# Attention scores as two products of 64 rows and 128 key columns each, with a reordered set-up

## The reference

```python
q = _split_heads(hidden_states @ w_q, HEADS)
k = _split_heads(text @ w_k, HEADS)
v = _split_heads(text @ w_v, HEADS)
out_text = _merge_heads(_sdpa(q, k, v))
mask_ip = _ip_mask(bbox, B, S, hidden_states.dtype)
k_ip = _split_heads(ip_h @ w_k_ip, HEADS)
v_ip = _split_heads(ip_h @ w_v_ip, HEADS)
out_ip = _merge_heads(_sdpa(q, k_ip, v_ip, mask=mask_ip))
out = (out_text + IP_SCALE * out_ip) @ w_out + b_out + residual
```

## Time and profile before

| | |
|---|---|
| median of 3 runs | 893.89 us (893.0 to 894.28) |
| the profiled execution's own time | 893.49 us |
| its span in the trace | 891.7 us |
| busy in the span: PE, PEld | 876.4 us, 749.5 us |
| busy: DVE, ACT, POOL | 725.7 us, 603.9 us, 540.6 us |
| instructions | 13892 |

### The profile page before, as it was taken

One profiled execution on the slowest core, in us unless ns is written; L12 is line 12 of the kernel. 1 busy time (PEld: TensorE's weight loads), 2 busy tenths in 40 slices (PEclk: granted clock), 3 DMA queues, 4 the chain that ended last, 5 costly groups with the idle time before them and its releaser, 6 DMA issues.

```text
span 891.7 us, 13892 instructions
## 1 busy us (share of the span) xinstructions
PE 876.4 (98%) x4685; PEld 749.5 (84%) x4685; DVE 725.7 (81%) x1006; ACT 603.9 (68%) x986; POOL 540.6 (61%) x431
## 2 busy tenths in 40 slices
PE   7999999999999999999999999999999999999988
PEld 6889788888888888888888888888888888888866
DVE  7959579787887979887897979888897979888784
ACT  7556486775758586675858587675858587675753
POOL 5349769284664839285664929375574929475561
PEclk9999999999999999999999999999999999999999
DMA  9843312203030301203030200303030210300011
GB/s 303 292 166 112 103 44 78 79 1 133 1 126 1 125 8 31 94 0 132 0 125 0 100 32 9 116 0 132 0 125 0 77 55 0 118 25 36 1 59 60
DMA packets 34059, 64.63 MB, mean 72 GB/s; under 512 B 4464, under 2 KB 6512, under 8 KB 33904
## 3 DMA queue, kind: packets, MB, share of 16 engines
q1 hardware_dynamic: 33888, 62.97, 21.0%
q10 hardware_dynamic: 144, 1.31, 0.3%
HBM read 40.34 MB, written 23.59 MB: 72 GB/s over the span
## 4 chain that ended last, share of the span: by engine, by line
PE 82%; DVE 4%; ACT 1%; POOL 1%; issue 0%; DVEq 0%
PE bank L95 23%; PE bank L97 22%; PE bank L96 22%; PE bank L1002 7%; PE bank L1011 4%; PE bank L1012 4%; DVE o_raw L905 1%; DVE res L912 1%; DVE total L223 1%; DVE pT_lo L898 1%; ACT oT_hi L820 0%; POOL prob L176 0%; ACT pv_part L816 0%; DVE prob L182 0%; DVE prob L176 0%
## 5 line engine op out<-in xcount | busy, mean ns | idle before, releaser
L765 POOL TENSOR_TENSOR oT_lo<-o_raw,oT_hi 128x512 fp32r<-128x512 f32 x80 | 103.5, 1293 | 244.1 <-ACT oT_hi L820 244.1
L176 POOL TENSOR_TENSOR prob<-prob,top 128x1120 f32<-128x1120 f32 x126 | 178.7, 1448 | 0.0
L182 POOL TENSOR_TENSOR prob<-prob,inv 128x1120 f32<-128x1120 f32 x126 | 174.1, 1414 | 0.2 <-DVE inv L225 0.2
L95 PE MATMUL bank<-xT_hi,wq_hi 128*128 128x512 f32 x400 | 163.3, 408 | 0.0
L97 PE MATMUL bank<-xT_hi,wq_lo 128*128 128x512 f32 x400 | 156.8, 392 | 0.0
L95 PE MATMUL bank<-oT_hi,wo_hi 128*128 128x512 f32 x400 | 156.2, 391 | 0.1
L96 PE MATMUL bank<-oT_lo,wo_hi 128*128 128x512 f32 x400 | 155.8, 389 | 0.0
L97 PE MATMUL bank<-oT_hi,wo_lo 128*128 128x512 f32 x400 | 155.7, 389 | 0.0
L96 PE MATMUL bank<-xT_lo,wq_hi 128*128 128x512 f32 x400 | 155.6, 389 | 0.0
L905 DVE TENSOR_TENSOR o_raw<-bank,pv_part 64x512 f32<-64x512 f32 x160 | 110.2, 689 | 50.7 <-ACT pv_part L816 48.2
L212 ACT ACTIVATE prob<-prob 128x1280 f32<-128x1280 f32 x64 | 81.6, 1276 | 79.7 <-POOL prob L176 79.6
(11 more groups left out here) (110 smaller groups left out, 1780.9 us busy)
## 6 DMA issues: line engine op xcount, KB each, us to landing
xin<-in_xT SPq DMA_DIRECT2D x16, 1280.0 KB, 6.8
outT<-res SPq DMA_DIRECT2D x80, 256.0 KB, 6.6
w_raw<-in_L_xattn_w_k SPq DMA_DIRECT2D x8, 320.0 KB, 5.6
w_raw<-in_L_xattn_w_k_ip SPq DMA_DIRECT2D x8, 320.0 KB, 5.5
w_raw<-in_L_xattn_w_v_ip SPq DMA_DIRECT2D x8, 320.0 KB, 3.1
w_raw<-in_L_xattn_w_v SPq DMA_DIRECT2D x8, 320.0 KB, 3.5
v_raw<-v_scratch SPq DMA_DIRECT2D x14, 140.0 KB
prob<-in_textT SPq DMA_DIRECT2D x8, 224.0 KB, 5.0
```

Of the source, the lines that this page charges most:

```text
L95: nc.tensor.matmul(dst, a_hi, b_hi, start=first, stop=False)
L176: ins = eng.tensor_tensor(s, s, top[:, t, n, :].unsqueeze(2).broadcast_to([P, HEADS, k1 - k0]), ALU.subtract)
L182: ins = eng.tensor_tensor(s, s, inv[:, t, n, :].unsqueeze(2).broadcast_to([P, HEADS, k1 - k0]), ALU.mult)
L765: nc.gpsimd.tensor_tensor(oT_lo[:, m, :], o_raw[:, m % 2, :], oT_hi[:, m, :].bitcast(F32), ALU.subtract).then_inc(oT_lo_done, 1)
```

## The change

The scores are made in two halves. A step's 128 rows are cut into rows 0 to 63 (heads 0 and 1 of the four) and 64 to 127 (heads 2 and 3). Each half is multiplied with only its own 128 key columns and writes a bank of its own, the two in turn. `k_hi` and `k_lo` become one tile `k_parts` [128, 5, 2 parts, 128 columns], of half the size. Four steps (`RUN`) fill one pair of banks, so PE's unit of work is now a pair of banks, five in a group (`score_units`), and ACT still copies ten banks of 512 columns, each into four strips of 128 columns of `prob` (`score_dst`). Pair u of 2 or more waits for `score_copied` of both banks of pair u-2. `units_for_tile` gives 4, 6, 8, 10 where it gave 3, 5, 8, 10.

In the set-up, PE does 20 transposes of the identity into bank 7 before its first wait for the context. The mask is split in two (`find_inside`, `make_mask`) and moved behind the low parts of query blocks 1 and 2; ACT's first copy of scores waits for it. Two of three `x_lo_part` of group 1 move behind the first and the second of the late weight chunks. POOL clears one key tile instead of two.

```diff
+    PW = 2 * KEYS
+    RUN = 512 // PW
...
-        k_hi, k_lo = sb("k_hi", [P, KD, HPT, KEYS], F32R), sb("k_lo", [P, KD, HPT, KEYS], F32R)
+        k_parts = sb("k_parts", [P, KD, 2, PW], F32R)
...
-            return -(-(t + 1) * SW // 512)
+            return 2 * -(-(t + 1) * KD // RUN)
...
-        def score_unit(pe, g, n, b, new_batch):
-            if n < 2:
+        def score_dst(n):
+
+            steps = prob[:, n // 2 * RUN * CW:(n // 2 + 1) * RUN * CW].rearrange("p (i r c) -> p r i c", r=2, c=PW)
+            return steps[:, n % 2, :, :]
+
+        def score_units(pe, g, u, b, new_batch):
+            if u == 0:
                 wait(pe, score_copied, UNITS * g)
-            elif n < 4:
+            elif u == 1:
                 wait(pe, pT_lo_done, PAIRS * g)
             else:
-                pe.wait_ge(score_copied, UNITS * g + n - 3)
-            if n == 0 and new_batch:
+                pe.wait_ge(score_copied, UNITS * g + 2 * u - 2)
+            if u == 0 and new_batch:
                 pe.wait_ge(k_built, HPT * (b + 1))
-            for half in range(2):
-                t, m = divmod(2 * n + half, KD)
+            for i in range(RUN):
+                t, m = divmod(RUN * u + i, KD)
                 if t == 0:
                     pe.wait_ge(q_lo_done, KD * g + m + 1)
                 q_cols = slice(t * P, (t + 1) * P)
-                keys = [k[:, m, :, :].rearrange("p j k -> p (j k)") for k in (k_hi, k_lo)]
-                ins = three(s_bank[n % 4][:, half * CW:(half + 1) * CW], qT_hi[:, m, q_cols], qT_lo[:, m, q_cols], *keys, True, True)
-            ins.then_inc(score_ready, 1)
...
+                for n, (q, part) in enumerate(((qT_hi, 0), (qT_hi, 1), (qT_lo, 0))):
+                    for r in range(2):
+                        rows = slice(r * HP, (r + 1) * HP)
+                        ins = nc.tensor.matmul(s_bank[(2 * u + r) % 4][:, i * PW:(i + 1) * PW], q[rows, m, q_cols], k_parts[rows, m, part, :], start=n == 0, stop=n == 2)
+                        if i == RUN - 1 and n == 2:
+                            ins.then_inc(score_ready, 1)
...
+                    act.wait_ge(mask_step, 6)
                     for u in range(UNITS):
                         copy_scores(act, 0, u)
...
-                            if k == KC - 3:
-                                make_mask()
...
                         q_lo_part(dve, 0, m)
+                        if m == 1:
+                            find_inside()
+                        elif m == 2:
+                            make_mask()
...
-                    for k in range(2, KD):
-                        x_lo_part(dve, 1, 1, k)
-                    for c in behind[4:]:
+                    x_lo_part(dve, 1, 1, 2)
+                    for n, c in enumerate(behind[4:]):
                         lo_chunk(c)
+                        if n < 2:
+                            x_lo_part(dve, 1, 1, 3 + n)
...
+                    pe.wait_ge(ident_made, 1)
+                    for n in range(20):
+                        nc.tensor.transpose(bank[7][:, 0:P], ident[:], ident[:])
```

More of the change, by code:

```diff
@@ L127, in q_lo_part, with k_head @@
             nc.vector.tensor_tensor(qT_lo[:, m, :], l_bank[(m + 1) % 2][:], qT_hi[:, m, :].bitcast(F32), ALU.subtract).then_inc(q_lo_done, 1)
-        def k_head(t, j):
-            return t[j * DH:(j + 1) * DH, :, j, :]
+        def k_head(part, j):
+            return k_parts[j * DH:(j + 1) * DH, :, part, j % 2 * KEYS:(j % 2 + 1) * KEYS]
         def k_hi_part(act, b, raw=None):
@@ L136, in k_hi_part @@
             for j in range(HPT):
-                nc.scalar.activation(k_head(k_hi, j), raw[j * DH:(j + 1) * DH], ACT.Copy).then_inc(k_hi_built, 1)
+                nc.scalar.activation(k_head(0, j), raw[j * DH:(j + 1) * DH], ACT.Copy).then_inc(k_hi_built, 1)
         def k_lo_part(dve, b, raw=None):
@@ L198, in score_unit, with copy_scores @@
                 q_cols = slice(t * P, (t + 1) * P)
-                keys = [k[:, m, :, :].rearrange("p j k -> p (j k)") for k in (k_hi, k_lo)]
-                ins = three(s_bank[n % 4][:, half * CW:(half + 1) * CW], qT_hi[:, m, q_cols], qT_lo[:, m, q_cols], *keys, True, True)
-            ins.then_inc(score_ready, 1)
-        def copy_scores(act, g, u):
-            act.wait_ge(score_ready, UNITS * g + u + 1)
-            nc.scalar.activation(prob[:, u * 512:(u + 1) * 512], s_bank[u % 4][:], ACT.Copy).then_inc(score_copied, 1)
+                for n, (q, part) in enumerate(((qT_hi, 0), (qT_hi, 1), (qT_lo, 0))):
[4 more added lines that the diff above has]
+                            ins.then_inc(score_ready, 1)
+        def copy_scores(act, g, n):
+            act.wait_ge(score_ready, UNITS * g + n + 1)
+            nc.scalar.activation(score_dst(n), s_bank[n % 4][:].rearrange("p (i c) -> p i c", c=PW), ACT.Copy).then_inc(score_copied, 1)
         def exponentials(act, g, t, shared):
@@ L386, in _ @@
                                             pattern=[[-1, P]], channel_multiplier=1).then_inc(ident_made, 1)
-                    for buf in (k_hi, k_lo):
-                        nc.gpsimd.memset(buf[:].rearrange("p m j k -> p (m j k)").bitcast(F32), 0.0).then_inc(k_zeroed, 1)
+                    nc.gpsimd.memset(k_parts[:].rearrange("p m s c -> p (m s c)").bitcast(F32), 0.0).then_inc(k_zeroed, 1)
                     mine = [c for c in range(len(chunks)) if c % 2 == 1]
@@ L516, in lo_chunk, with step, find_inside @@
                         nc.vector.tensor_tensor(lo, w_raw[:, c % LOADS, :], hi.bitcast(F32), ALU.subtract).then_inc(w_lo_done[0], 1)
[L518 to L524, removed]
+                    def step(ins, n):
+                        ins.then_inc(mask_step, 1)
+                        dve.wait_ge(mask_step, n)
+                    def find_inside():
                         def edge(f, cols=None):
@@ L534, in make_mask @@
                         nc.vector.tensor_tensor(inside_y[:, 0, :, :], y_all, edge(1, TPB), ALU.is_ge)
[L535 to L537 removed]
+                        step(nc.vector.tensor_tensor(inside_y[:, 1, :, :], y_all, edge(3, TPB), ALU.is_le), 1)
+                        step(nc.vector.tensor_tensor(inside_x[:, 0, :], inside_x[:, 0, :], inside_x[:, 1, :], ALU.mult), 2)
+                        step(nc.vector.tensor_tensor(inside_y[:, 0, :, :], inside_y[:, 0, :, :], inside_y[:, 1, :, :], ALU.mult), 3)
                         ins_all = inside[:].rearrange("p b m t -> p (b m) t")
[L539 to L540 removed]
+                        nc.vector.tensor_tensor(ins_all, inside_y[:, 0, :, :], inside_x[:, 0, :].unsqueeze(2).broadcast_to([P, B * BOXES, TPB]), ALU.mult).then_inc(mask_step, 1)
+                    def make_mask():
+                        dve.wait_ge(mask_step, 4)
+                        step(nc.vector.tensor_reduce(any_in, inside[:].rearrange("p b m t -> p b t m"), AX.X, ALU.max), 5)
                         mask_b = mask[:].rearrange("p (b t) k -> p b t k", b=B)
@@ L544, in make_mask @@
                             last = nc.vector.tensor_scalar(mask_b[:, :, :, BOXES + n], inside[:, :, n, :], 1.0, -NEG, ALU.subtract, ALU.mult)
-                        step(last)
+                        last.then_inc(mask_step, 1)
                     mine = [c for c in range(len(chunks)) if c % 2 == 0]
@@ L679, in _ @@
                             ins.then_inc(k_ipT_ready, 1)
-                    for n in range(UNITS):
-                        score_unit(pe, 0, n, 0, True)
+                    for u in range(UNITS // 2):
+                        score_units(pe, 0, u, 0, True)
                     for k in range(KC):
@@ L1038, in scores @@
                 def scores(g, b, new_batch, more):
-                    for n in range(UNITS):
-                        score_unit(pe, g, n, b, new_batch)
+                    for u in range(UNITS // 2):
+                        score_units(pe, g, u, b, new_batch)
                     for m in range(KD):
```

4 lines of the change are left out of this document (2 added, 2 removed).

## The result

| | before | after |
|---|---|---|
| median | 893.58 us (893.0 to 897.21, 20 runs) | 894.89 us (894.39 to 895.76, 20 runs) |
| profiled execution, its span | 893.49 us, 891.7 us | 894.63 us, 892.8 us |

The ratio is 1.0013 with a 95% interval of 1.0007 to 1.0019: 1.3 us slower, where 890.0 and a gain were forecast. The time lies inside the range of 866 to 900, and inside the 0.2% that the prediction called no difference, but the interval shows a small loss.

What follows compares the result with a forecast made beforehand. PE, busy 98% of the span, was taken as the bound. From the profiled 893.5 us, 0.5 for the halves and 3.4 for the set-up gave 889.6; with the median 0.4 above, 890.0 us, range 866 to 900.

Steps and rivals of the forecast that it cites:

- The pace of a pair: PE's scores: time from one pair of half matmuls to the next, taken as 0.11 us, against 0.120 per matmul before.
- (d): Rival on PE's scores: full doubling, a pair every 0.06 us, ACT's copies bind, 866.5 us; chance 0.12.
- (c): Rival on PE's scores: pairs at the old pace of 0.12 us, 0.36 more a group, 896.3 us; chance 0.15.
- (b): Rival on PE's scores: loads of the halves run one after the other, 0.22 us a pair, 991 us; chance 0.22.
- Going in and out: PE entering and leaving 64-row matmuls around the scores: 0.29 us extra a group, lower bound 0.
- the waits for copies: PE's score pairs waiting for ACT to copy banks: 0.06 and 0.21 us, 0.27 a group.
- the halves bring 0.03 a group: Score stage on PE: 7.16 us a group against 7.19, a gain of 0.5 us in 16 groups.
- The chain ends 0.36 later, and 1.09 was there.: Softmax chain: POOL's mask of tile 2 starts 0.36 us later, inside POOL's 1.09 us lead over PE's transposes.
- The set-up: Before group 0: 2.0 us from an earlier quick pace and 1.4 from late weights, 3.4 gained, bounds 0 and 3.6.
- The late weights: Set-up: two subtractions of x moved behind DVE's low part of weights, which PE awaits 1.41 us; 1.4 us gained.
- Rival (a): Rival on the set-up: the transposes don't raise the clock, 2.0 us are missing, 892.0 us; chance 0.15.
- The prediction's rival on the other side: PE's scores: loads one after the other, 6.3 us more a group, 991 us; chance 0.22.

Runs made afterwards that it cites:

- half of the terms: Changed kernel without the two low-order products of rows 64 to 127, four matmuls a step instead of six; 957.79 us in one run.
- Keys late: Changed kernel with DVE's next-batch key subtractions moved behind the low parts of the first two query blocks and two pT_part; 891.14 us, ratio 0.9969 to the kernel before.
- halves in turn: Changed kernel with three matmuls of one half issued, then three of the other, in each step; 894.52 us in one run.
- the set-up alone: Kernel before with only the set-up edits (20 transposes, mask and two x subtractions moved), scores as before; 890.37 us, ratio 0.9962.
- the halves alone: Changed kernel with the set-up of before, so only the scores in halves; 898.03 us, ratio 1.0046 to the kernel before.

## Why the prediction went wrong

**The pace of a pair was right**, 0.112 us for 0.11. The bounds of 0.06, 0.12 and 0.22, rivals (d), (c) and (b), are all out. Loads of the two halves run side by side, a load of 64 rows is recorded as long as one of 128 (0.19 us), and the work of one half binds (half of the terms); that its loads are what binds is the prediction's reason, and nothing here speaks against it. The Trainium skill (TensorEngine Tiling (Array Packing), Key Properties) says that different tiles can execute weight loads and matmuls in parallel; the trace agrees, with two loads within 0.19 us. It gains nothing more here, since each half has to load as often as the whole did.

**Going in and out, and the waits for copies.** 0.29 + 0.27 a group were forecast. The waits are 0.05 and 0.16 in group 5, 0.2 in all. Going in costs 327.31 - 326.99 = 0.32 against a pace of 0.23, and the first pairs stand 0.05 further apart; leaving costs 0.09 and 0.10: 0.34 together. With 20 steps of 0.335, 6.70 where 6.60 were forecast, the sum is 7.2. From steady matmul to steady matmul it is 7.70 less two steps of 0.23, 7.24, where the earlier trace rows have 7.19 and the forecast 7.16. So "the halves bring 0.03 a group" should have read: they cost 0.05, 0.8 us in 16 instead of 0.5 gained. It is a term mis-sized by 1.3 us: the edges (0.34 for 0.29) and a pace of 0.112 for 0.110 sixty times over add 0.15 a group, the waits take back 0.06.

**The failed step** is "The chain ends 0.36 later, and 1.09 was there." The 0.36 was right (0.40). The cover of 1.09 is that of POOL's scaling before PE's transposes in group 5, and in groups 1 to 14 it held: PE has no wait for `prob` there. It failed in two ways. The same 0.36 moves DVE's sums, DVE's order puts four key subtractions and then `qT_lo` behind them, and in seven groups PE was already late by that, 0.13 us each; the 0.37 more in each are 2.6 us. And in the last group there was no cover: PE waited 0.32 for POOL and now waits 0.64, and the end comes 0.35 later. With the 0.05 of the halves themselves in 15 groups (0.8) these make 3.7 of the 3.9 us lost behind the set-up. The rest lies in the groups without new keys, which are 0.10 longer and not 0.05; the new waits for `res` of DVE stand there, but no run priced them. So from the first transposes on the kernel lost 3.9 where 0.5 less was forecast, 4.4 of the 5.0 us between the 889.6 forecast for the profiled execution and its 894.63; the set-up is the other 0.6. Keys late takes the wait for `qT_lo` away and gets 3.75 us back, of which 7 x 0.50 = 3.5 are priced by the groups.

**The set-up** was right in kind. 2.8 us came of 3.4. The quick pace came at 7.3 instead of 6.9, and the transposes brought 1.2 us where 2.0 were counted: 12 slow matmuls were to be saved, but between the two set-ups, with and without the transposes, it was 2.7 us of slow time (7.6 against 10.3), 7 matmuls at 0.16 each. The 5.3 us of work that stood ahead of the quick pace in the kernel before is no constant: in the other traces it was 3.1 (halves in turn) to 6.1 us (the set-up alone). The mask, which the sum put at nothing, brought some of the rest: PE stands 1.7 us ahead of the kernel before at the end of the first 15 matmuls and 2.5 ahead at about 64 us, before the late weights. The late weights brought some 0.4 instead of 1.4: PE begins them 1.4 us earlier, and then waits 0.74 for POOL's low part, which was hidden behind DVE's. Rival (a), that the transposes don't raise the clock, fell. The Trainium skill (TensorE: Matmul & The Clock Gate, PE-mode transpose) says that transposes don't count as busy in the same way; here the measurement decides otherwise, quick pace at 7.6 with 20 of them ahead and at 10.3 without, and in halves in turn at 4.6, among the transposes themselves.

**The chances.** The case that came was the forecast one in its mechanism, with an addition that none of the rivals named. The prediction's rival on the other side needed a mishap on PE; the one that happened was 0.36 us of delay on an engine that looked 81% busy. That 894.89 lies inside the range, and nearer to the 896.3 of rival (c) than to the forecast, is luck: (c) asked for pairs at 0.12, and they went at 0.112.

**Open.** In the profiled executions two kernels with halves have short stretches at a lower clock that the others don't show: 0.83 in 90 to 100 us and 0.84 in 860 to 870 us of the halves alone, 0.85 in 860 to 870 us of keys late. Over all executions with both halves at full work, 9 of 37 have a mean granted clock of 0.998 or less; of the 46 with the scores in one piece none has. So the stretches come with the halves, though why isn't shown. They don't explain the loss: the profiled execution of the changed kernel kept 1.00, and its four executions at 0.998 (894.5 to 895.35) are no slower than the others. In the halves alone the two such executions are the slowest of five (898.83 and 900.27), so there they may cost something.

## What to carry to other kernels

A cover belongs to one pair of engines and to one kind of group; the last group, with less work ahead of the same wait, may have none. When a chain ends later, follow every consumer of it, engine by engine and in each kind of group, to the work that stands behind it in a fixed order; the row to look for is the instruction that starts just as its input is ready, with no wait shown yet. Work that is needed a stage later (here the next batch's keys) should not stand ahead of work that another engine is about to need. Splitting a matmul's rows gained little here, 0.112 us for 0.120, since every half needs its own loads, and going in and out cost more than that.

## What the runs showed of the hardware

- Two fp32r matmuls of 64 rows and 128 columns in different row halves and banks, with their loads, take 0.112 us a pair. Their order in the queue, in turn or three and three, changes nothing, and taking away two of one half's three changes nothing either (0.335 us for three in all three kernels).
- Where one half of the rows did a third of its matmuls (one execution), the granted clock fell below 0.8 in some 10 us of nearly every group, to 0.50 at the end of the score stage shown, and 957.8 us were measured for less work. The profiled execution of the changed kernel, with both halves working, kept 1.00. An experiment that takes work off PE can be slower by the clock alone, so its clock is to be read before its time.
- DVE's subtraction of 32 x 320 elements took 1.04 us on average, 0.49 to 2.25, while POOL was scaling (28 in 29.1 us) and 0.48 where it was moved to (28 in 13.5 us), without any edit to it. Moving work on DVE can change its length as well as its place.
- Twenty fp32 transposes of an identity from 1.52 us on brought PE to its quick pace at 7.6 us or earlier in seven traces; in three kernels without them it came at 10.1 to 11.3 us.
